# A new order of work, and one scaling moved to ScalarE, in a two-part image block on one NeuronCore

## The chip, the cores and the metric

One core of a Trainium2 chip runs the whole program. The metric is the device time of one execution in microseconds (us), lower is better.

## The reference

The input `x` holds 8 images of 256 channels by 32 x 32 pixels, in fp32. Each image goes through two parts, and images don't depend on one another.

```
conv part:   n   = (x - mean over channels) / sqrt(var + 1e-6)
             qkv = W_qkv n                                  (768 rows)
             agg = pointwise(depthwise 5x5(qkv))            (768 rows)
             per head of 8 rows, raw qkv and agg alike:
               q, k = relu(...);  kv = k^T [v, 1];  out = (q kv) / (q k^T 1)
             y   = x + batchnorm(W_proj out)
token part:  t   = layernorm of y over channels, per pixel
             w   = expert weights of the image: mean over pixels -> router -> softmax -> top 2
             out = y + sum_e w_e (gelu(t W1_e + b1_e) W2_e + b2_e)   (6 experts of width 341)
```

So the expert weights `w` of an image need its whole conv part, its second norm and a small router, and no second product of the token part can be made without them.

## The kernel before

Channels lie on the 128 partitions, an image is two tiles of 1024 pixels. The 768 rows of qkv are six tiles: 0 and 1 are q, 2 and 3 are k, 4 and 5 are v.

**Engines.** TensorE (PE) does every product. fp32 precision in the large products comes from splitting both sides into an fp16 high part and an fp16 low part: three fp16 products in place of one. ScalarE (ACT) empties every PSUM bank of the products, one by one. VectorE (DVE) does the depthwise 5x5 convolution as "taps", one SCALAR_TENSOR_TENSOR for each of most taps and each tile, in the tile order (2, 3), (4, 5), (0, 1): 132 operations for the first image, 138 for each other one. The remaining ("base") taps of a tile are scaled by ACT and added by GpSimd (POOL, L875 and L881). POOL also does the norms' sums, reciprocal roots and products, the scaling of the attention output, the low parts, and additions into the output. SyncE (SP) loads and stores.

**Order.** `schedule()` writes one list of items, `ORDER`, and PE, ACT, POOL and SP each walk it from front to back and do their part of each item, with semaphores between them. So an item that waits on one engine holds back everything behind it on that engine. Two PSUM banks take turns: a product may fill a bank only when ACT has emptied the product two places before. The items of one image are:

- `squares`, `sums`, `stats`, `rnorm`, `rbc`, `apply`, `high`, `low`: a norm (number 0 of the input, 1 of the token part), with two tiles or two halves each. `stats` are 32 PE products of one column, `rbc` spreads the result to all partitions, `apply` multiplies on POOL, `high` and `low` split the result.
- `qkv`: tile and pixel half. `base`: a base tap. `agg`: the pointwise product after the taps.
- `tok` (transposes of raw k and v), `kv`, `mask`, `att`, `scale`, `back`: the attention, half 0 from raw qkv, half 1 from the aggregated tiles. `proj`: the projection with the addition to `x`.
- `logits`, `exp`: the router. `ffn`: the first product of one of 32 feed-forward blocks (2 pixel halves by 16 groups of 128 hidden rows), with gelu. `gsplit`: the hidden rows times their expert weight, split into high and low. `second`: the second product of a block, `LAG` = 3 blocks behind its `ffn`. `final`: what a pixel half gives to the output.

DVE doesn't walk the list. It runs the taps of all images, and between taps with certain numbers it does small tasks: the reciprocals of the attention's denominators (`rden`), and the router's maximum (`max`) and expert weights (`route`). Each waits for other engines, and the taps behind it wait too:

```
OF_LAST = {14: ("rden", 1, 0), 20: ("rden", 1, 1), 74: ("max",), 84: ("route",)}
OF_THIS = {94: ("rden", 0, 0), 100: ("rden", 0, 1)}
```

OF_LAST belongs to the image before the one whose taps run, OF_THIS to that image itself. A period here is the time from the `agg` of tiles 0 and 1 of one image to that of the next. In a middle period (image number j), the list before holds, in short: agg of tiles 0, 1; attention half 1; qkv tiles 0, 1 of the next image; proj; tok; second norm; kv and mask; logits; then the input norm of the next image, attention half 0, agg and qkv of tiles 2 to 5 and kv half 1. Of the 32 ffn blocks of each period 15 stand ahead of the logits and 17 behind.

Of the kernel before, what the change touches and what calls it, by code (L numbers as in the profile page):

```python
# [31 lines left out]
P = 128  # L32
B, C, HH, WW = 8, 256, 32, 32
T = HH * WW
CT = C // P
# [44 lines left out]
def schedule():  # L80

    o = []
    waiting = []
    stream = [(s, f) for s in range(B) for f in range(NCH * FT)]
    todo = list(stream)
    given = set()

    def give(it):
        o.append(it)
        given.add(it)  # L90
# [7 lines left out]
    def fill(k, s):  # L98
        for _ in range(k):
            if not todo or todo[0][0] > s:  # L100
                return
            i = len(stream) - len(todo)
            n = todo.pop(0)
            assert ("low", n[0], 1) in given
            give(("ffn",) + n)
            if i > 0:
                assert ("exp", stream[i - 1][0]) in given
                give(("gsplit",) + stream[i - 1])
            if i >= LAG:
                second(i - LAG)  # L110

    def based(items, n=1):
        for it in items:
            give(it)
            for b in waiting[:n]:
                give(b)
            del waiting[:n]

    def rest():
        for b in waiting:  # L120
            give(b)
        waiting.clear()

    def qkv(s, a, n=1):
        for m in (a, a + 1):
            based([("qkv", s, m, c) for c in range(NCH)], n)
            waiting.extend(("base", s, m, i) for i in range(base_taps(s, m)))

    def agg(s, a, n=1):
        based([("agg", s, m, c) for m in (a, a + 1) for c in range(NCH)], n)  # L130

    for j in range(-1, B + 2):
        d, c, a = 0 <= j < B, 1 <= j <= B, 0 <= j + 1 < B
        old, new = j - 2, j - 1
        n = 3 if j == 0 else 1
        if c:
            agg(new, 0)
            fill(1, old)
            for t in range(TT):
                based([("att", new, 1, t)])  # L140
                if t % 2:
                    fill(1, old)
            give(("scale", new, 1))
        if d:
            qkv(j, 0, n)
        if c:
            fill(1, old)
            based([("back", new, 1, ch, g) for ch in range(NCH) for g in range(2)])
            fill(1, old)
            based([("proj", new, ch, m) for ch in range(NCH) for m in range(CT)])  # L150
            give(("squares", new, 1))
            give(("sums", new, 1))
        if d:
            give(("relu_q", j))
            for t in range(TT):
                based([("tok", j, t)], n)
                if t % 2:
                    fill(1, old)
        if c:
            based([("stats", new, 1, 0)])  # L160
            give(("rnorm", new, 1))
            fill(2, old)
            based([("rbc", new, 1, ch) for ch in range(NCH)])
            give(("apply", new, 1))
            fill(2, old)
            give(("high", new, 1))
            give(("low", new, 1))
        if d:
            based([("kv", j, 0, g) for g in range(2)], n)
            give(("mask", j, 0))  # L170
        if c:
            based([("logits", new)])
        fill(NCH * FT, old)
        if a:
            give(("squares", j + 1, 0))
            give(("sums", j + 1, 0))
        if j == -1:
            give(("weights", 0))
        if c:
            give(("exp", new))  # L180
        fill(2, new)
        if a:
            based([("stats", j + 1, 0, i) for i in range(2)])
            give(("rnorm", j + 1, 0))
            fill(2, new)
            based([("rbc", j + 1, 0, ch) for ch in range(NCH)])
            give(("apply", j + 1, 0))
        if j == -1:
            give(("weights", 1))
        if d:  # L190
            for t in range(TT):
                based([("att", j, 0, t)], n)
                if t % 2:
                    fill(1, new)
            give(("scale", j, 0))
        if a:
            give(("high", j + 1, 0))
            give(("low", j + 1, 0))
        fill(2, new)
        if d:  # L200
            based([("back", j, 0, ch, g) for ch in range(NCH) for g in range(2)], n)
            rest()
            agg(j, 2)
            fill(1, new)
        if a:
            qkv(j + 1, 2)
            fill(1, new)
        if d:
            agg(j, 4)
            fill(1, new)  # L210
        if a:
            qkv(j + 1, 4)
            fill(1, new)
        if d:
            based([("kv", j, 1, g) for g in range(2)])
            give(("mask", j, 1))
        rest()
    k = len(stream)
    assert not todo
# [5 lines left out]

ORDER = schedule()
# [16 lines left out]
def norm_before():  # L243

    runs = [(it[1], it[2]) for it in ORDER if it[0] == "squares"]
    return dict(zip(runs[1:], runs))
# [22 lines left out]
def build(nc, x, w_qkv, w_dw, w_pw, w_proj, bn, bn_rows, w_router, w1, b1, w2, b2, parts, out):  # L269
    with ExitStack() as ctx:  # L270
# [134 lines left out]
        def drained(it):  # L405

            return FILL[it] + 1
# [723 lines left out]
```

## Time and profile before

| | |
|---|---|
| median of 3 runs | 1727.04 us (1724.31 to 1729.64) |
| the profiled execution | 1725.51 us, of which 1723.6 us span |
| instructions | 18116 |
| busy, PE | 1403.7 us (81%) |
| busy, DVE | 1303.4 us (76%) |
| busy, POOL | 1187.4 us (69%) |
| busy, ACT | 915.0 us (53%) |
| mean granted TensorE clock | 0.90 of full speed |
| load of one image, issue to landing | 5.0 us (median) |

The span runs from the first to the last instruction. A busy time is the time in which the engine had at least one instruction running. The granted clock has two levels, full (2.4 GHz) and half (1.2 GHz), and a stretch shows their mean. L487 and L500 are the lines of the split products (`ffn` and `qkv`; `second`), L534 and L539 those of `agg`, L1067 that of the taps.

### The profile page before, as it was taken

How to read it: one execution, taken by the hardware profiler on the slowest of the kernel's cores; microseconds unless marked ns; L12 is line 12 of the kernel's file. 1: busy time of each engine (PE TensorE's matmuls, PEld its weight loads, DVE VectorE, ACT ScalarE, POOL GpSimd, SP SyncE). 2: the span in 40 equal slices, each digit the busy share in tenths (PEclk: the TensorE clock that was granted, in tenths of full speed). 3: DMA queues.
4: the chain of work that ended last, by engine and by line, in shares of the span. 5: the costliest groups of instructions: out<-in, count | busy, mean ns of one | idle time of the engine just before them, and what ended most of it. 6: DMA issues, size and time to landing. Idle time of an engine off the chain costs nothing.

```text
span 1723.6 us, 18116 instructions
## 1 busy us (share of the span) xinstructions
PE 1403.7 (81%) x6652; PEld 771.5 (45%) x6652; DVE 1303.4 (76%) x1305; ACT 915.0 (53%) x1606; POOL 1187.4 (69%) x1017
## 2 busy tenths in 40 slices
PE   4344865988889878988889878988889879768998
PEld 2133534544545435544545435544445435534443
DVE  4999999889589895889589895889589895920000
ACT  3452642565557644665557645565557645433554
POOL 3673554877697758876697758876697757535776
PEclk7666986999999989999999989999999989988999
DMA  5100000000010000100010000100010000100000
GB/s 173 74 0 25 1 0 0 25 1 13 1 62 1 13 1 0 62 1 13 1 60 3 13 1 1 61 1 13 1 37 1 13 0 1 37 0 13 1 13 25
DMA packets 14247, 32.70 MB, mean 19 GB/s; under 512 B 2384, under 2 KB 5328, under 8 KB 13904
## 3 DMA queue, kind: packets, MB, share of 16 engines
q1 hardware_dynamic: 14160, 31.56, 5.2%
q8 instruction: 52, 0.85, 0.2%
q14 instruction: 35, 0.29, 0.1%
HBM read 23.17 MB, written 8.39 MB: 18 GB/s over the span
## 4 chain that ended last, share of the span: by engine, by line
PE 44%; DVE 23%; POOL 16%; ACT 10%; issue 6%; DMA 1%; POOLq 0%; SPq 0%; DVEq 0%
DVE dacc L1067 19%; PE wbk L487 16%; PE acc L500 12%; PE wbk L580 6%; POOL dwo L881 4%; POOL gl L915 3%; POOL hb L912 3%; ACT tapb L655 2%; POOL yr L905 2%; PE wbk L589 2%; PE wbk L534 2%; POOL nrm L838 1%; PE wbk L539 1%; PE wbk L554 1%; PE wbk L566 1%
## 5 line engine op out<-in xcount | busy, mean ns | idle before, releaser
L1067 DVE SCALAR_TENSOR_TENSOR dacc<-qkvs,dww,dacc 128x930 f32<-128x930 f32 (+4 forms) x954 | 1052.3, 1185 | 0.0
L912 POOL TENSOR_SCALAR hb<-hb,ewg 128x512 f32<-128x512 f32 x256 | 189.8, 742 | 252.2 <-ACT gh L677 252.1
L915 POOL TENSOR_TENSOR gl<-hb,gh 128x512 f16<-128x512 f32 x256 | 306.3, 1196 | 21.4
L770 ACT ACTIVATE hb<-wbk,b1s 128x512 f32<-128x512 f32 x256 | 175.4, 686 | 244.4 <-PE wbk L487 243.8
L881 POOL TENSOR_TENSOR dwo<-dwo,tapb 128x992 f32<-128x992 f32 (+1 forms) x104 | 237.4, 2283 | 46.7 <-ACT tapb L655 39.5
L487 PE MATMUL wbk<-th,w1h 128*128 128x512 f16 x512 | 163.8, 403 | 69.7 <-ACT vt L743 36.7
L500 PE MATMUL acc<-gh,w2h 128*128 128x512 f16 x512 | 200.6, 392 | 19.4 <-POOL gl L915 19.3
L677 ACT ACTIVATE gh<-hb,ewg 128x512 f16<-128x512 f32 x256 | 182.3, 712 | 40.7 <-DVE ewg L1020 40.7
L500 PE MATMUL acc<-gl,w2h 128*128 128x512 f16 x512 | 200.0, 391 | 0.0
L500 PE MATMUL acc<-gh,w2l 128*128 128x512 f16 x512 | 199.8, 390 | 0.0
L487 PE MATMUL wbk<-tl,w1h 128*128 128x512 f16 x512 | 162.3, 400 | 0.0
L487 PE MATMUL wbk<-th,w1l 128*128 128x512 f16 x512 | 160.7, 397 | 0.0
L655 ACT ACTIVATE tapb<-qkvs,dww 128x1024 f32<-128x1024 f32 x104 | 118.0, 1144 | 72.8 <-POOL dwo L881 66.6
L977 DVE MAX8 mx<-lg 128x8 f32<-128x16 f32 x8 | 1.4, 176 | 168.2 <-ACT lg L767 168.2
L971 DVE RECIPROCAL den<-den 128x128 f32<-128x128 f32 x32 | 30.4, 951 | 98.0 <-ACT den L750 97.6
L487 PEld LDWEIGHTS wbk<-th,w1h 128*128 128x128 f16 x512 | 42.6, 102 | 133.6 <-ACT vt L743 42.3
L500 PEld LDWEIGHTS acc<-gh,w2h 128*128 128x128 f16 x512 | 51.4, 100 | 91.0 <-POOL gl L915 29.3
L487 PE MATMUL wbk<-xh,wqh 128*128 128x512 f16 x192 | 59.0, 390 | 40.7 <-ACT qkvs L727 20.9
L534 PE MATMUL wbk<-dwo,pw 128*128 128x512 f32 x64 | 44.4, 836 | 53.5 <-ACT qr L734 32.4
L727 ACT ACTIVATE qkvs<-wbk 128x512 f32<-128x512 f32 x96 | 56.9, 593 | 53.0 <-PE wbk L487 52.8
L861 POOL TENSOR_TENSOR kt<-kt,den 128x1024 f32<-128x1024 f32 x32 | 62.5, 1971 | 32.3 <-DVE den L971 32.3
L487 PEld LDWEIGHTS wbk<-tl,w1h 128*128 128x128 f16 x512 | 52.5, 102 | 67.9 <-issue 13.2
(147 smaller groups left out, 2388.7 us busy)
## 6 DMA issues: line engine op xcount, KB each, us to landing
xa<-x SPq DMA_DIRECT2D x8, 1024.0 KB, 5.0
yr<-x SPq DMA_DIRECT2D x8, 1024.0 KB, 5.0
out<-yr SPq DMA_DIRECT2D x16, 512.0 KB, 2.8
dwo<-w SPq DMA_DIRECT2D x1, 2048.0 KB, 10.9
yr<-w SPq DMA_DIRECT2D x2, 1024.0 KB, 16.0
dwo<-w_qkv SPq DMA_DIRECT2D x1, 768.0 KB, 4.7
wp<-w_proj SPq DMA_DIRECT2D x1, 512.0 KB, 12.1
pw<-w_pw SPq DMA_DIRECT2D x16, 24.0 KB
```

What stands on the lines that cost most here:

```text
L487: last = nc.tensor.matmul(dst, w[:, k, m * P:(m + 1) * P], d[:, k, c * CH:(c + 1) * CH], start=(i == 0), stop=(i == len(parts) - 1))
L500: last = nc.tensor.matmul(acc[:, m, :], w[:, t, m * P:(m + 1) * P], d[:, f % GB, :], start=(t == 0 and i == 0), stop=(t == FT - 1 and i == 2),
L534: last = nc.tensor.matmul(b[:], pw[:, m, :], dwo[:, m, c * CH:(c + 1) * CH], start=True, stop=True)
L580: last = nc.tensor.matmul(b[:], wp[:, k, m * P:(m + 1) * P], (ac, qr)[k // CT][:, k % CT, c * CH:(c + 1) * CH], start=(k == 0), stop=(k == ...
L655: ins = nc.scalar.activation(tapb[:, i % 2, :], qkvs[:, m, :], ACT.Copy, scale=w)
L677: nc.scalar.activation(gh[:, f % GB, :], hb[:, f % GB, :], ACT.Copy, scale=w).then_inc(g_high, 1)
L770: last = nc.scalar.activation(hb[:, f % GB, :], b[:], ACT.Gelu, bias=b1s[:, f % FT:f % FT + 1], scale=1.0 / (X_SCALE * W_SCALE))
L861: nc.gpsimd.tensor_tensor(v, v, r, ALU.mult).then_inc(att_scaled[h], 1)
L881: ins = nc.gpsimd.tensor_tensor(d3[:, oy, ox], d3[:, oy, ox], t3[:, iy, ix], ALU.add)
L912: nc.gpsimd.tensor_scalar(hb[:, f % GB, :], hb[:, f % GB, :], ewg[s % 2][:, f % FT:f % FT + 1], 0.0, ALU.mult, ALU.add).then_inc(g_scaled, 1)
L915: nc.gpsimd.tensor_tensor(gl[:, f % GB, :], hb[:, f % GB, :], gh[:, f % GB, :], ALU.subtract).then_inc(g_low, 1)
L1067: ins = nc.vector.scalar_tensor_tensor(out=dst[:, oy, ox], in0=i3[:, jy, jx], scalar=dww[:, m, tap:tap + 1], in1=a3[:, oy, ox], op0=ALU.mu ...
```

## The change

The list is written anew. DVE's tasks move to other tap numbers, `high`, `low`, `squares`, `relu_q`, `apply` and `scale` become items of one tile or half, and one operation changes its engine.

1. The tapped image's way to its routing goes ahead. Of the 32 blocks of a period 9 stand ahead of the logits (5 of them between `agg` and `proj`, where 7 stood) and 23 behind. The loop keeps `KEEP` = 9 blocks of an image for the next period.
2. Attention half 0 of the image whose taps run, up to its `att`, `scale` and the items beside them, and `qkv` tile 2 of the next image move ahead of the logits. `back` of half 0 stands right behind them.
3. The input norm is begun two images ahead of the tapped one, where it was one ahead: `squares` to `apply` stand between the first blocks after `exp`, each group with one block, and `high` and `low` wait until the next period, beside `proj` and `tok`. In the first image the norm of image 1 stands among the base taps, ahead of attention half 0.
4. After the logits two blocks stand ahead of `exp`, then `agg` of tiles 2, 3. One block stands between single `agg`, `qkv`, `kv` and base items.
5. `gsplit`: POOL's multiplication of `hb` by the expert weight (L912) goes to ACT, behind the one that makes `gh`. POOL keeps the subtraction (L915).
6. DVE's tasks: `rden` of half 1 at taps 10 and 14, `rden` of half 0 at 58 and 64, `max` at 72, `route` at 80.

```diff
+    def give(*items, n=1):
+        for it in items:
+            o.append(it)
+            given.add(it)
+            if it[0] in BANKED and n > 1:
+                base(n)
+    def base(n):
+        o.extend(waiting[:n])
+        del waiting[:n]
+    def rest():
+        base(len(waiting))
+    def add_base(s, a):
+        waiting.extend(("base", s, m, i) for m in (a, a + 1) for i in range(base_taps(s, m)))
...
+    def fill(k):
         for _ in range(k):
...
+            if todo and ("low", todo[0][0], 1, CT - 1) in given and (("exp", todo[0][0]) in given or todo[0][1] < 2):
+                i = len(stream) - len(todo)
+                give(("ffn",) + todo.pop(0))
+                while unsplit and ("exp", unsplit[0][0]) in given:
+                    give(("gsplit",) + unsplit.pop(0))
+                unsplit.append(stream[i])
+                if i >= LAG:
+                    second(i - LAG)
+            base(1)
...
+    def norm_in(s):
+        return [[("squares", s, 0, 0)], [("squares", s, 0, 1), ("sums", s, 0)],
+                [("stats", s, 0, 0)], [("stats", s, 0, 1), ("rnorm", s, 0)],
+                [("rbc", s, 0, 0), ("rbc", s, 0, 1)], [("apply", s, 0, 0)], [("apply", s, 0, 1)]]
+    def norm_out(s):
+        return [[("high", s, 0, 0)], [("low", s, 0, 0), ("high", s, 0, 1)], [("low", s, 0, 1)]]
...
+    for j in range(B + 1):
+        d, c, a, f = j < B, j >= 1, j + 1 < B, j + 2 < B
+        new, nxt = j - 1, j + 1
         n = 3 if j == 0 else 1
         if c:
...
+            give(*agg(new, 0), *agg(new, 1))
+            fill(1)
             for t in range(TT):
...
+                give(("att", new, 1, t))
+                if t == 3:
+                    fill(1)
+                    give(("scale", new, 1, 0))
+            give(("scale", new, 1, 1))
+        if j == 0:
+            for group in norm_in(1)[:2]:
+                give(*group)
         if d:
...
+            give(*qkv(j, 0), *qkv(j, 1), n=n)
+            add_base(j, 0)
+            if j == 0:
+                for group in norm_in(1)[2:]:
+                    give(*group, n=n)
+        out = norm_out(nxt) if a else [[], [], []]
         if c:
...
+            fill(2)
+            give(*[("back", new, 1, ch, g) for ch in range(NCH) for g in range(2)])
+            fill(1)
+            give(("proj", new, 0, 0), *out[0])
+            give(("proj", new, 0, 1))
+            give(("proj", new, 1, 0), *out[1])
+            give(("proj", new, 1, 1))
+        else:
+            give(*out[0], *out[1])
+        toks = [("tok", j, t) for t in range(TT)] if d else []
+        give(*toks[:2], n=n)
+        if c:
+            if not d:
+                fill(2)
+            give(*out[2], ("squares", new, 1, 0))
+            give(*toks[2:4])
+            give(("squares", new, 1, 1), ("sums", new, 1))
+            give(*toks[4:])
+        else:
+            give(*out[2], *toks[2:], n=n)
         if d:
...
+            give(("relu_q", j, 0))
+            give(("kv", j, 0, 0), ("kv", j, 0, 1), n=n)
+            give(("mask", j, 0), ("relu_q", j, 1))
         if c:
...
+            fill(1)
+            give(("stats", new, 1, 0), ("rnorm", new, 1))
+            fill(1)
         if d:
...
+            give(*[("att", j, 0, t) for t in range(4)], n=n)
         if c:
...
+            fill(1 if d else 2)
+            give(("rbc", new, 1, 0), ("rbc", new, 1, 1), ("apply", new, 1, 0), ("apply", new, 1, 1))
+        if d:
+            give(("scale", j, 0, 0))
+            give(*[("att", j, 0, t) for t in range(4, TT)], n=n)
         if c:
+            give(("high", new, 1, 0))
+            fill(1 if d else 2)
+            give(("high", new, 1, 1))
+        if d:
+            give(("scale", j, 0, 1))
+        if c:
+            give(("low", new, 1, 0), ("low", new, 1, 1))
+            if a:
+                give(*qkv(nxt, 2))
+            give(("logits", new))
+        if d:
+            give(*[("back", j, 0, ch, g) for ch in range(NCH) for g in range(2)], n=n)
+        if c:
+            if a:
+                give(*qkv(nxt, 3))
+            else:
+                fill(1)
+            fill(left(new - 1) + 2)
             give(("exp", new))
...
+        rest() if j == 0 else None
         if d:
...
+            give(*agg(j, 2), *agg(j, 3))
+            if a and c:
+                add_base(nxt, 2)
+        if j == 0:
+            give(*qkv(1, 2), *qkv(1, 3))
+            add_base(1, 2)
         if d:
...
+            for group in norm_in(j + 2) if f else [[]] * 4:
+                give(*group)
+                fill(1)
+            fill(1)
+            give(*agg(j, 4))
+            fill(1)
+            give(*agg(j, 5))
+            fill(1)
+            if a:
+                for m in (4, 5):
+                    for it in qkv(nxt, m):
+                        give(it)
+                        fill(1)
+                add_base(nxt, 4)
+            else:
+                fill(4)
+            give(("kv", j, 1, 0))
+            fill(2)
+            give(("kv", j, 1, 1))
+            fill(1)
             give(("mask", j, 1))
...
+            while left(new) > KEEP and new >= 0:
+                fill(1)
...
+KEEP = 9
...
                     nc.scalar.activation(gh[:, f % GB, :], hb[:, f % GB, :], ACT.Copy, scale=w).then_inc(g_high, 1)
+                    nc.scalar.activation(hb[:, f % GB, :], hb[:, f % GB, :], ACT.Copy, scale=w).then_inc(g_scaled, 1)
...
-                    pool.wait_ge(g_high, no)
-                    pool.sem_inc(pool_gate, 1)
-                    nc.gpsimd.tensor_scalar(hb[:, f % GB, :], hb[:, f % GB, :], ewg[s % 2][:, f % FT:f % FT + 1],
-                                            0.0, ALU.mult, ALU.add).then_inc(g_scaled, 1)
                     pool.wait_ge(g_scaled, no)
...
-            OF_LAST = {14: ("rden", 1, 0), 20: ("rden", 1, 1), 74: ("max",), 84: ("route",)}
-            OF_THIS = {94: ("rden", 0, 0), 100: ("rden", 0, 1)}
+            OF_LAST = {10: ("rden", 1, 0), 14: ("rden", 1, 1), 72: ("max",), 80: ("route",)}
+            OF_THIS = {58: ("rden", 0, 0), 64: ("rden", 0, 1)}
```

## Rows read from the trace of the kernel before

**Rows 1.** The page's part 4, the chain of work that ended last, by engine.
```profile
PE 44%; DVE 23%; POOL 16%; ACT 10%; issue 6%; DMA 1%; POOLq 0%; SPq 0%; DVEq 0%
```

**Rows 2.** Windows: us, then busy us of each engine (instructions), PEclk, DMA share, GB/s.
```profile
754.60:949.10 194.50, 171.08 (x831) 93.34 (x830) 161.97 (x162) 111.67 (x199) 145.80 (x125) 0.94 0.05 17
...
1338.20:1519.30 181.10, 141.41 (x699) 78.98 (x697) 155.83 (x160) 88.28 (x167) 110.98 (x102) 0.91 0.04 12
...
1519.30:1723.60 204.30, 184.62 (x794) 87.47 (x794) 5.52 (x21) 95.50 (x160) 137.59 (x135) 0.94 0.03 11
```

**Rows 3.** Timeline of PE: start, us, line, operation, [idle before <-releaser].
```profile
202.06 1.96 PE L534 MATMUL wbk<-dwo,pw 128*128 128x512 f32 x4 [2.19 <-DVE dwo L1053]
...
366.23 1.88 PE L534 MATMUL wbk<-dwo,pw 128*128 128x512 f32 x4
...
754.58 1.88 PE L534 MATMUL wbk<-dwo,pw 128*128 128x512 f32 x4
...
761.57 3.78 PE L534 MATMUL wbk<-dwo,pw 128*128 128x512 f32 x4 [5.11 <-ACT qr L734]
...
859.66 0.51 PE L599 MATMUL wbk<-rws,us 128*128 128x11 f32 x4
...
1519.26 6.51 PE L534 MATMUL wbk<-dwo,pw 128*128 128x512 f32 x8 [18.93 <-DVE dwo L1053]
```

**Rows 4.** Timeline of DVE in the period from 754.6 us.
```profile
775.14 6.70 DVE L1067 SCALAR_TENSOR_TENSOR dacc<-qkvs,dww,dacc 128x961 f32<-128x961 f32 x6
...
813.00 28.78 DVE L1067 SCALAR_TENSOR_TENSOR dacc<-qkvs,dww,dacc 128x900 f32<-128x900 f32 x26
...
860.53 0.18 DVE L977 MAX8 mx<-lg 128x8 f32<-128x16 f32 x1 [18.75 <-ACT lg L767]
...
861.07 11.10 DVE L1067 SCALAR_TENSOR_TENSOR dacc<-qkvs,dww,dacc 128x961 f32<-128x961 f32 x10
...
880.47 4.40 DVE L1067 SCALAR_TENSOR_TENSOR dacc<-qkvs,dww,dacc 128x930 f32<-128x930 f32 x4
```

**Rows 5.** Groups of one period: xcount | busy, mean ns | idle before.
```profile
L677 ACT ACTIVATE gh<-hb,ewg 128x512 f16<-128x512 f32 x32 | 22.8, 713 | 5.4 <-DVE ewg L1020 5.4
...
L912 POOL TENSOR_SCALAR hb<-hb,ewg 128x512 f32<-128x512 f32 x32 | 24.1, 752 | 27.9 <-ACT gh L677 27.9
...
L915 POOL TENSOR_TENSOR gl<-hb,gh 128x512 f16<-128x512 f32 x32 | 38.7, 1210 | 2.7
...
L881 POOL TENSOR_TENSOR dwo<-dwo,tapb 128x992 f32<-128x992 f32 x12 | 27.5, 2295 | 5.6 <-ACT tapb L655 5.0
...
L566 PE MATMUL wbk<-kvm,qr 128*128 128x144 f32 x64 | 9.5, 289 | 0.1
...
L554 PE MATMUL wbk<-vt,kt 128*128 128x129 f32 x64 | 7.5, 275 | 0.0
...
L547 PE MATMUL wbk<-ident,qkvs 128*128 128x128 f32 x32 | 4.5, 277 | 0.3 <-ACT sum_b L756 0.3
```

**Rows 6.** The chain of the same period in order of time: start, us.
```profile
823.39 2.74 PE wbk L487 x6
...
831.40 1.29 PE acc L500 x6
...
840.61 3.46 PE wbk L589 x32
...
884.37 1.65 POOL sv L826
```

**Rows 7.** Timelines of DVE and POOL in the first two images.
```profile
118.25 37.34 DVE L1067 SCALAR_TENSOR_TENSOR dacc<-qkvs,dww,dacc 128x900 f32<-128x900 f32 x34
...
124.51 0.45 POOL L851 TENSOR_TENSOR kvm<-kvr,blk 128x128 f32<-128x128 f32 x1 [7.27 <-ACT kvr L745]
...
285.69 11.09 DVE L1067 SCALAR_TENSOR_TENSOR dacc<-qkvs,dww,dacc 128x961 f32<-128x961 f32 x10
...
300.00 4.40 DVE L1067 SCALAR_TENSOR_TENSOR dacc<-qkvs,dww,dacc 128x930 f32<-128x930 f32 x4
```

More of the change, by code:

```diff
@@ L96, in second @@
             give(("final", s, n // FT))
-    def fill(k, s):
+    def fill(k):
         for _ in range(k):
[L100 to L130, printed above, removed]
@@ new lines, in norm_out @@
+    def norm_out(s):
+        return [[("high", s, 0, 0)], [("low", s, 0, 0), ("high", s, 0, 1)], [("low", s, 0, 1)]]
+    give(("squares", 0, 0, 0), ("squares", 0, 0, 1), ("sums", 0, 0), ("weights", 0), ("stats", 0, 0, 0),
+         ("stats", 0, 0, 1), ("rnorm", 0, 0), ("rbc", 0, 0, 0), ("rbc", 0, 0, 1), ("apply", 0, 0, 0),
+         ("apply", 0, 0, 1), ("weights", 1), ("high", 0, 0, 0), ("low", 0, 0, 0), ("high", 0, 0, 1), ("low", 0, 0, 1))
+    give(*[it for m in range(2, QT) for it in qkv(0, m)])
@@ L135, in schedule @@
+    add_base(0, 2)
+    add_base(0, 4)
+    for j in range(B + 1):
+        d, c, a, f = j < B, j >= 1, j + 1 < B, j + 2 < B
+        new, nxt = j - 1, j + 1
         n = 3 if j == 0 else 1
         if c:
-            agg(new, 0)
-            fill(1, old)
+            give(*agg(new, 0), *agg(new, 1))
+            fill(1)
             for t in range(TT):
[L140 to L143, printed above, removed]
@@ L144, in schedule @@
-        if d:
-            qkv(j, 0, n)
-        if c:
[L147 to L152, printed above, removed]
-        if d:
[L154 to L158, printed above, removed]
@@ L159, in schedule @@
-        if c:
[L160 to L167, printed above, removed]
+                give(("att", new, 1, t))
[3 more added lines that the diff above has]
+            give(("scale", new, 1, 1))
@@ L179, in schedule @@
-        if c:
-            give(("exp", new))
[L181 to L189, printed above, removed]
-        if d:
[L191 to L199, printed above, removed]
-        if d:
[L201 to L215, printed above, removed]
+            fill(1 if d else 2)
@@ L223, in schedule @@
     return o
+KEEP = 9
+BANKED = ("qkv", "agg", "kv", "stats", "rbc", "att", "back", "proj", "tok", "logits", "ffn")
 ORDER = schedule()
-BANKED = ("qkv", "agg", "kv", "stats", "rbc", "att", "back", "proj", "tok", "logits", "ffn")
 FILL = {it: n for n, it in enumerate([it for it in ORDER if it[0] in BANKED])}
@@ L243, in norm_before @@
 def norm_before():
-    runs = [(it[1], it[2]) for it in ORDER if it[0] == "squares"]
+    runs = [(it[1], it[2]) for it in ORDER if it[0] == "squares" and it[3] == 0]
     return dict(zip(runs[1:], runs))
@@ L441, in _ @@
             for it in ORDER:
[L442 removed]
+                if it[0] == "apply" and it[2:] == (0, CT - 1) and it[1] + 1 < B:
                     s = it[1]
```

107 lines of the change are left out of this document (48 added, 59 removed).

## The prediction

> **What bounds the kernel now.** I read the chain first, then windows of one period each, then the timelines. The chain [rows 1] changes hands: PE holds 44% of it, DVE 23%, POOL 16%, ACT 10%. No engine is the bound by itself, and a period is a loop of waits. The windows say the same [rows 2]: in a middle period of 194.5 us PE is busy 171.1 us, DVE 162.0, POOL 145.8, ACT 111.7, at a mean granted clock of 0.94. The starts of the agg of tiles 0 and 1 [rows 3] give the frame: image 0 at 202.1, image 1 at 366.2, then steps of 194.5 (949.1 in rows 2), then 181.1 for the last to 1519.3, and 204.3 to the end.
>
> Where the loop is closed shows in DVE's timeline [rows 4]. MAX8 at 860.5 waited 18.8 us for the logits, which PE made at 859.7, 105 us after its agg at 754.6 [rows 3]. Ten taps follow (11.1 us), and the route block lasts until 880.5, 8.3 us. ACT's gsplit waits for it (5.4 us in the row of L677 [rows 5]), and with it the second products. From there to the next agg it is 68.6 us. So 105 + 21 + 69 us is the period: whoever shortens the way from agg to logits gains until another wait ends last.
>
> **Prices.** Six matmuls of 512 columns take 1.29 us at the full clock, so a block (ffn and second) takes PE 2.58 us, and a qkv chunk 1.29 [rows 6]. At the half level, after PE stood idle, the same six take 2.74 with their end [rows 6]. An fp32 pass of four instructions takes 1.88 us with its end, some 1.72 without [rows 3]: agg of tiles 0 and 1 is 3.8 us, proj eight such, 13.8. A norm's stats take 3.5 us [rows 6]; the attention's products 9.5 us for 16 att, 7.5 for both kv, 4.5 for 8 tok, so 2.3 for four back [rows 5].
>
> **The scaling on ACT.** It isn't in the trace. The nearest row is the gh operation on the same tile, 0.71 us [rows 5]; its bounds are 0.6 (overlap with its neighbours) and 0.75 (what POOL took). It adds 32 x 0.65 = 21 us to ACT's 112 in a period, and takes 24 from POOL's 146. ACT at 133 us of some 187 is not the bound. What it buys lies elsewhere: a block's way from gelu to gl is as long as before (0.71 + 1.16 in place of 0.75 + 1.21), but POOL gets free in a crowded stretch.
>
> **From agg to DVE's task at tap 58.** Ahead of the first four att of half 0 PE has, in the new list: agg 3.8, 7 blocks 18.1, 12 att 7.1, 4 qkv chunks 5.2, back 2.3, proj 13.8, tok 4.5, kv 3.7 (one half), stats 3.5. Sum 62.0. Waits: two PSUM banks and ACT's queue ahead of back (gelu, gh, the new scaling, a base tap) 2; ahead of tok's third the squares, which now wait for low of the next image: proj's last drain and addition, then a low on POOL like an add of L881 (2.3 us [rows 5]), then two squares between the tok drains: 6, and 1 for the clock; 1 for the last drain. So these att are drained 72 us after the agg. DVE is there earlier: it waits at tap 10 for the attention half 1 until 9.6, and then has 4 taps, two reciprocals and 44 taps, which is tap 58 at 64 (taps 14 to 74 take 66.6 in rows 4, from 775.1 to 841.8). It waits 8 us.
>
> **From tap 58 to the weights.** 1.0 (reciprocal) + 6.7 (6 taps) + 1.0 + 8.9 (8 taps) puts the maximum at 89.6 us; the logits are ready by my count at 86 (two more blocks, norm product, high, two qkv chunks), so their 18.8 us of waiting are gone. Then 0.5 + 8.9 (8 taps) + the route block. It took 8.3 us in rows 4 and 3.3 us in image 0 (296.8 to 300.0 [rows 7]), where POOL had no work in it; in the middle periods POOL was in the norm's sums. In the new list those stand behind gsplit, which needs the weights, so POOL is idle there: I take 3.4, with 8.3 as the other end. Weights at 102.4 us, against 126 before. *The port.* The Trainium skill (SBUF — State Buffer, Who interferes with whom) says that VectorE's tensor_scalar in its two-port mode, or an operation with two SBUF inputs, and a GpSimd operation that reads SBUF shut each other out for a whole instruction. By it the block would be 3.3 us with POOL idle and about 8.3 with POOL in long operations; the two blocks of this trace agree.
>
> **From the weights to the next agg.** Before PE's first second product with them come gh, hb and gl: 2.7 us. Then 39 half blocks 50.3, stats 3.5, rbc (one pass) 1.7, agg of tiles 4 and 5 taken as that of 0 and 1, 3.8, 4 qkv chunks 5.2, kv 3.7: 68.2. POOL has two gl (2.4), two output additions of half a tile (about half of an L881 add each, 2.5) and the norm's sums (two of that size, 4.7 [rows 5]) ahead of stats: they end 8.8 us after the weights, where PE is at 4.0: 4.8 of waiting. Then POOL has a gl and a base add (2.3) with each block, 3.5 us against PE's 2.6, and rnorm (1.65 for the power [rows 6], a product of full size and three small steps, 4.6): rbc waits some 4. These two gaps put the clock down: 2 + 2.6. Sum 2.7 + 68.2 + 4.8 + 4 + 4.6 = 84.3. The period is 102.4 + 84.3 = 186.7; bounds 178 (POOL's two waits hidden) and 195 (route block 8.3, and 3 us more for handovers).
>
> **The ends.** *Image 0:* DVE was busy through it. Its attention half 0 was done long ahead of tap 94; now tap 58, at about 122.7 [rows 7], needs it. The mask came at 124.5, after 7.3 us of waiting for kv [rows 7], so POOL was done with the base adds at 117.2. It now has the next image's norm among and behind them: sums 4.7, rnorm 4.6, apply (two products like an add of L881) 4.7, which makes 131.2, then high 1. Only then come tok and kv, with nothing else for PE and so at the half clock, 7 and 6.5: I get the mask at 147 and the att at 151, so DVE waits 28 us: agg at 230, not 202 (bounds 0 and 35). *Period 1* holds 23 blocks behind its weights instead of 14. DVE has no wait ahead of them: 84 + 0.5 + 8.9 + 3.4 = 97, + 84.3 = 181: 411. *Periods 2 to 5:* 4 x 186.7 = 747: 1158. *Period 6* has no input norm: 5.2 of PE's work, its two waits and their clock go, 102.4 + 2.7 + 63 + 1 = 169: 1327. *Period 7* has no qkv either (5.2) and no low ahead of tok (6): 96 + 2.7 + 58 = 157, which is also DVE's own work (162 less the 5 of the route block); with handovers 160: 1487, against 1519. *The end:* 204.3 us with 54 blocks to finish; now 41. 13 x 2.58 = 33.5 less, but the last image's chain has 9 blocks of cover for 22, and the weights come when no block is left: + 7 there (route after exp, 5 us, and the clock 2). 178: 1665.
>
> Span 1665, and 1.9 between span and time as in the profiled execution, whose 1725.5 is 1.5 under the median of the runs: **1667 us**, 3.5% faster.
>
> **DMAs.** Each input load is issued behind the last apply of its image and waited for a whole period later; the output stores and loads stand at their old places by the final items. They cost nothing while a load (5.0 us to landing in the table ahead) has more than 100 us of cover.
>
> **The rivals.** *A, the covers work:* sums, rnorm and apply on POOL end in time, and PE doesn't wait there. For it speaks that POOL loses 24 us a period, against it the count above. 178 in 4 periods and 173 in the first: 1667 - 35 - 8 = 1624. *B, only the ends gain:* the route block stays at 8.3 and each handover of two banks costs 0.2 more: period 195, + 33 + 8: 1708. *C, slower:* the attention of the tapped image is late for tap 58. Each us that it is later than my 72 is a us of all of periods 1 to 5, since nothing else of the loop is slack there but PE, which waits too. The 60 us of gain are used up by 12 us a period: att drained at 84 decides. Fifteen us late would give 1742. For it: the chain ACT to POOL to ACT at tok is new, and PE at half the clock would make 62 us of work longer quickly; against it: before, the logits, which lie behind more work, took 105. *D, nothing changes* (within 0.3%, which is about what a measurement of this kernel can tell from no change): gains and the new waits of image 0 and period 1 (+28, +17) cancel.
>
> *The clock.* Before, PE's row at 823.4 shows half-level durations behind an idle stretch [rows 6], and the period's mean is 0.94; I expect 0.93 to 0.96. The Trainium skill (TensorE: Matmul & The Clock Gate, HAM oscillation) warns that idle gaps which recur with each tile cost the slow start each time; it would speak for C, and the rows price a start at 2 to 3 us.
>
> **How the numbers follow.** Forecast (1635 to 1690) 0.55, A 0.15, B 0.18, C 0.09, D 0.03. The range holds forecast, A and B with their bounds: 1612 to 1715. Faster 0.88, same 0.03, slower 0.09.
>
> **What would show it.** Right: MAX8 waits under 2 us and the rden at tap 58 about 8; the route block 3.4 us; PE waits for POOL at stats and rbc in the middle of a period; DVE waits some 28 us at tap 58 of image 0; 41 blocks behind the last agg. Wrong: a rden wait over 20 us in each period (C), no POOL waits of PE (A), or the route block at 8 us (B). What would most easily make the number wrong is the handovers between ACT and PE, of which I count only the large ones.

## The result, and the profile after

The changed kernel takes 1746.78 us (median of 4 runs, 1745.71 to 1749.76) against 1727.11 for the kernel before in the same comparison: 1.0117 times as long, with a 95% interval of 1.0097 to 1.0137. I had forecast 1667. The profiled execution has a span of 1745.5 us, 21.9 more than before, and a mean granted clock of 0.894.

The page's part 4, and three groups of its part 5:

```profile
PE 43%; POOL 26%; ACT 11%; DVE 11%; issue 8%; DMA 1%; POOLq 0%; SPq 0%; ACTq 0%; DVEq 0%
...
L956 POOL TENSOR_TENSOR gl<-hb,gh 128x512 f16<-128x512 f32 x256 | 302.3, 1183 | 493.2 <-ACT hb L725 492.5
...
L1012 DVE RECIPROCAL den<-den 128x128 f32<-128x128 f32 x32 | 30.5, 952 | 269.6 <-ACT den L798 269.3
...
L725 ACT ACTIVATE hb<-hb,ewg 128x512 f32<-128x512 f32 x256 | 182.0, 711 | 0.0
```

Beside [rows 1] the chain has lost half of DVE (23% to 11%) and has gained as much of POOL (16% to 26%), although POOL does less work in all than before (1005.5 us busy for 1187.4). The group of L1012 shows that DVE now waits 270 us in the run for the attention, where it waited 98 before.

Windows of the changed kernel: a middle period, its parts up to the weights and behind them, and the last three periods (the columns are those of [rows 2]):

```profile
816.70:1018.10 201.40, 175.42 (x829) 98.21 (x828) 158.95 (x161) 130.98 (x232) 123.76 (x93) 0.92 0.05 16
816.70:923.30 106.60, 96.65 (x458) 57.46 (x457) 84.39 (x93) 66.77 (x136) 60.95 (x43) 0.92 0.00 1
923.30:1018.10 94.80, 78.77 (x373) 40.75 (x372) 74.56 (x69) 64.21 (x97) 62.81 (x50) 0.93 0.09 34
...
1219.50:1404.20 184.70, 165.31 (x794) 91.61 (x793) 159.85 (x161) 126.91 (x226) 113.39 (x84) 0.94 0.03 12
1404.20:1572.10 167.90, 153.14 (x745) 86.12 (x744) 146.02 (x151) 109.27 (x204) 84.48 (x69) 0.94 0.04 13
1572.10:1745.50 173.40, 150.79 (x639) 71.80 (x638) 5.42 (x21) 103.25 (x176) 83.47 (x66) 0.93 0.03 9
```

The middle period is 201.4 us, not the 186.7 of the forecast, and not the 194.5 of before [rows 2]. PE does the same products in it, but is busy 4.3 us longer and idle 2.6 us longer (26.0 for 23.4). The extra busy time is matmuls at the half clock: the mean granted clock of the period fell from 0.94 to 0.92, which is some 4 us of 200 (an estimate from these two figures).

By periods, from one agg of tiles 0 and 1 to the next:

| stretch | before | forecast | measured |
|---|---|---|---|
| to the agg of image 0 | 202.1 | 230 | 230.8 |
| to that of image 1 | 164.1 | 181 | 183.1 |
| four middle periods, each | 194.5 | 186.7 | 201.4 |
| the next | 194.5 | 169 | 184.7 |
| the last | 181.1 | 160 | 167.9 |
| the end | 204.3 | 178 | 173.4 |

Against before the first two cost 48 us and the middle 28, and the last three give back 54. Against the forecast nearly everything is in the middle: 59 of the 80 us, and 16 and 8 in the two periods behind it, which are built alike.

PE in the changed kernel, at its starts of agg (230.80, 413.89, 816.71) and at its larger waits of the middle period (the bracket is the idle time before the row and what ended it):

```profile
230.80 4.39 PE L582 MATMUL wbk<-dwo,pw 128*128 128x512 f32 x5 [23.10 <-DVE dwo L1094]
...
413.89 2.40 PE L582 MATMUL wbk<-dwo,pw 128*128 128x512 f32 x5
...
816.71 3.69 PE L582 MATMUL wbk<-dwo,pw 128*128 128x512 f32 x8
...
867.27 4.01 PE L595 MATMUL wbk<-ident,qkvs 128*128 128x128 f32 x16 [3.08 <-ACT vt L791]
872.12 5.93 PE L602 MATMUL wbk<-vt,kt 128*128 128x129 f32 x32 [0.84 <-ACT vt L791]
...
929.28 0.38 PE L548 MATMUL acc<-gh,w2h 128*128 128x512 f16 x1 [2.86 <-ACT sum_b L758]
...
934.80 3.55 PE L637 MATMUL wbk<-mean_w,rb 128*128 128x1 f32 x16 [4.07 <-POOL rb L858]
...
942.35 1.84 PE L637 MATMUL wbk<-mean_w,nrm 128*128 128x1 f32 x16
...
951.09 3.22 PE L643 MATMUL wbk<-rb,spread 128*128 128x512 f32 x4 [4.28 <-POOL rb L876]
...
1012.53 0.39 PE L548 MATMUL acc<-gh,w2h 128*128 128x512 f16 x1 [2.43 <-POOL gl L956]
```

The price of a wait shows twice: the bracket is the wait itself, and the row shows what follows it at the half clock. Stats take 3.55 us at 934.8 for the 1.84 of the second sixteen at 942.4, rbc 3.22 for 1.88, kv 5.93 for 3.7.

DVE in the changed kernel:

```profile
149.64 0.95 DVE L1012 RECIPROCAL den<-den 128x128 f32<-128x128 f32 x1 [29.85 <-ACT den L798]
...
825.85 0.95 DVE L1012 RECIPROCAL den<-den 128x128 f32<-128x128 f32 x1 [29.39 <-ACT den L798]
...
892.90 0.95 DVE L1012 RECIPROCAL den<-den 128x128 f32<-128x128 f32 x1 [12.12 <-ACT den L798]
...
910.19 0.17 DVE L1018 MAX8 mx<-lg 128x8 f32<-128x16 f32 x1
...
919.98 0.16 DVE L1027 RECIPROCAL rt<-rt 128x1 f32<-128x1 f32 x1 [0.36 <-ACT rt L751]
...
923.31 8.84 DVE L1108 SCALAR_TENSOR_TENSOR dacc<-qkvs,dww,dacc 128x930 f32<-128x930 f32 x8
...
934.62 5.53 DVE L1100 SCALAR_TENSOR_TENSOR dacc<-qkvs,dww,dwo 128x1024 f32<-128x1024 f32 x2
...
986.62 2.49 DVE L1100 SCALAR_TENSOR_TENSOR dacc<-qkvs,dww,dwo 128x1024 f32<-128x1024 f32 x2
```

The 18.8 us at MAX8 [rows 4] are gone and the route block is 3.3 us (919.98 to 923.31), so the weights come 106.6 us after the agg, where it was 126. But at 825.85 DVE has a wait of 29.4 us for half 1 that was 5.7 before: it has run ahead and waits one agg later. That is the first sign that its wait isn't what closes the loop.

### The profile page after: what moved, and what is told of

Read it like the earlier page. It is cut to its first block, busy times and chain, and to the rows that moved or that the text cites. A ratio compares the mean times of both kernels' runs of the same rounds, so it can differ in the third digit from the quotient of the medians.

```text
span 1745.5 us, 17861 instructions
## 1 busy us (share of the span) xinstructions
PE 1427.3 (82%) x6652; PEld 797.3 (46%) x6652; DVE 1285.1 (74%) x1305; ACT 1070.7 (61%) x1863; POOL 1005.5 (58%) x761
## 4 chain that ended last, share of the span: by engine, by line
PE 43%; POOL 26%; ACT 11%; DVE 11%; issue 8%; DMA 1%; POOLq 0%; SPq 0%; ACTq 0%; DVEq 0%
PE wbk L535 16%; PE acc L548 10%; DVE dacc L1108 8%; POOL dwo L926 8%; POOL gl L956 5%; PE wbk L628 5%; PE wbk L602 4%; POOL nrm L885 3%; PE wbk L637 2%; ACT hb L725 2%; ACT gh L724 2%; ACT hb L818 1%; PE wbk L587 1%; PE wbk L582 1%; POOL kt L906 1%
## 5 line engine op out<-in xcount | busy, mean ns | idle before, releaser
L956 POOL TENSOR_TENSOR gl<-hb,gh 128x512 f16<-128x512 f32 x256 | 302.3, 1183 | 493.2 <-ACT hb L725 492.5
L818 ACT ACTIVATE hb<-wbk,b1s 128x512 f32<-128x512 f32 x256 | 175.4, 685 | 184.3 <-PE wbk L535 183.8
L926 POOL TENSOR_TENSOR dwo<-dwo,tapb 128x992 f32<-128x992 f32 (+1 forms) x104 | 241.7, 2324 | 15.1 <-ACT tapb L703 12.1
L1012 DVE RECIPROCAL den<-den 128x128 f32<-128x128 f32 x32 | 30.5, 952 | 269.6 <-ACT den L798 269.3
L725 ACT ACTIVATE hb<-hb,ewg 128x512 f32<-128x512 f32 x256 | 182.0, 711 | 0.0
L643 PE MATMUL wbk<-rb,spread 128*128 128x512 f32 x64 | 44.0, 825 | 57.6 <-POOL rb L876 57.6
L1100 DVE SCALAR_TENSOR_TENSOR dacc<-qkvs,dww,dwo 128x1024 f32<-128x1024 f32 x46 | 90.3, 2006 | 0.0
L614 PE MATMUL wbk<-kvm,qr 128*128 128x144 f32 x512 | 80.4, 301 | 9.1 <-ACT rb L813 3.2
L595 PE MATMUL wbk<-ident,qkvs 128*128 128x128 f32 x256 | 49.8, 348 | 42.3 <-ACT vt L791 37.3
## 6 DMA issues: line engine op xcount, KB each, us to landing
wp<-w_proj SPq DMA_DIRECT2D x1, 512.0 KB, 12.1
```

The source lines that it names most:

```text
L614: last = nc.tensor.matmul(b[:, g * RD:(g + 1) * RD], qr[:, g, t * P:(t + 1) * P], kvm[:, g, :], start=True, stop=True)
L725: nc.scalar.activation(hb[:, f % GB, :], hb[:, f % GB, :], ACT.Copy, scale=w).then_inc(g_scaled, 1)
L818: last = nc.scalar.activation(hb[:, f % GB, :], b[:], ACT.Gelu, bias=b1s[:, f % FT:f % FT + 1], scale=1.0 / (X_SCALE * W_SCALE))
L926: ins = nc.gpsimd.tensor_tensor(d3[:, oy, ox], d3[:, oy, ox], t3[:, iy, ix], ALU.add)
L956: nc.gpsimd.tensor_tensor(gl[:, f % GB, :], hb[:, f % GB, :], gh[:, f % GB, :], ALU.subtract).then_inc(g_low, 1)
L1100: ins = nc.vector.scalar_tensor_tensor(out=dacc[:, m % 2, :], in0=qkvs[:, m, :], scalar=w, in1=dwo[:, m, :], op0=ALU.mult, op1=ALU.add)
```

## Experiments

**Theory 1:** PE's own list closes the period. Its length is PE's work, plus each wait in the list, plus the half-clock stretch behind each wait; DVE and the weights have slack. **Theory 2** (rival C of the prediction): the late attention half 0 holds DVE at tap 58, and DVE's wait holds the agg.

**1. Later DVE tasks.** The changed kernel with later tap numbers:

```diff
-OF_LAST = {..., 72: ("max",), 80: ("route",)}
-OF_THIS = {58: ("rden", 0, 0), 64: ("rden", 0, 1)}
+OF_LAST = {..., 76: ("max",), 84: ("route",)}
+OF_THIS = {66: ("rden", 0, 0), 72: ("rden", 0, 1)}
```

> Only DVE's task numbers move: rden of half 0 from taps 58 and 64 to 66 and 72, max from 72 to 76, route from 80 to 84. DVE's wait for the attention (12.1 us in each middle period of the changed kernel) shrinks to about 3 us. Theory 1 (what sets the time of the weights is exp on ACT, which stands behind two blocks and ends at 919.9 us when DVE's tap 80 is at 919.6; DVE's wait costs nothing by itself): weights at the same time after the agg (106.6 us), whole time the same within 0.3%, 1742 to 1752. Theory 2 (rival C of the prediction taken by itself: each us of waiting at tap 58 is a us of the period): 9 us less in five periods, 1702 or less.

Measured: 1751.68 us, 1.0143 times the time before (1.0111 to 1.0175). The same three waits of DVE in this kernel:

```profile
828.45 0.95 DVE L1012 RECIPROCAL den<-den 128x128 f32<-128x128 f32 x1 [37.81 <-ACT den L798]
...
895.02 0.95 DVE L1012 RECIPROCAL den<-den 128x128 f32<-128x128 f32 x1 [2.76 <-ACT den L798]
...
909.30 0.18 DVE L1018 MAX8 mx<-lg 128x8 f32<-128x16 f32 x1 [1.27 <-ACT lg L815]
```

The wait of 12.1 us fell to 2.8 and the one at half 1 grew from 29.4 to 37.8. The period did not shrink (202.5), and the time stayed in theory 1's range. Theory 2 falls.

**2. Weights earlier as well.** The same, with the router's exp ahead of its two blocks:

```diff
-            fill(left(new - 1) + 2)
-            give(("exp", new))
+            fill(left(new - 1))
+            give(("exp", new))
+            fill(2)
```

> The late tap numbers, and exp ahead of the two blocks that stand between logits and exp. Theory 1 (exp behind blocks on ACT is late): the weights come 5 to 6 us earlier after the agg, near 101 us. If PE's way behind the weights starts with them, each of five periods gains 5 us: 1720. If POOL's sums of the next norm bound that way and can't start earlier, the gain stays under 2 us a period: 1737 or more. Theory 2 (DVE's wait at tap 58): no more than with the late tap numbers alone, 1702.

Measured: 1748.40 us, 1.0137 (1.0111 to 1.0164). The weights came at 103.5 us, 3 earlier than in the changed kernel and not the 5 to 6 forecast; the stretch behind them, which now has the two blocks in it, grew from 94.7 to 97.9, and the period stayed at 201.4. So the weights don't close the loop either: only the division of PE's list by them has moved.

**3 and 4. The two halves of the change.** Number 3 is the changed kernel with the scaling on POOL again. Number 4 is the kernel before with the scaling on ACT and nothing else:

```diff
                     nc.scalar.activation(gh[...], hb[...], ACT.Copy, scale=w).then_inc(g_high, 1)
+                    nc.scalar.activation(hb[...], hb[...], ACT.Copy, scale=w).then_inc(g_scaled, 1)
...
-                    pool.wait_ge(g_high, no)
-                    pool.sem_inc(pool_gate, 1)
-                    nc.gpsimd.tensor_scalar(hb[...], hb[...], ewg[...], 0.0, ALU.mult, ALU.add).then_inc(g_scaled, 1)
```

> The scaling of hb goes back from ACT to POOL, everything else as changed. Theory 1 (behind the weights POOL is the bound with gl, sums, base adds and rnorm): POOL has 0.7 us more per block in that stretch, 6 blocks up to rbc, 4 to 8 us a period more, 1770 to 1790. Theory 3 (the loss comes from ACT, which carries 21 us more in a period and empties banks later): the kernel gets faster than 1747, at least down to the time before, 1727.

> The kernel before with the scaling of hb on ACT alone. Theory 1: POOL's queue ahead of the agg and behind it (base adds behind gsplit) gets shorter, ACT is at 133 of 194 us: faster by 1 to 4 us a period, 1700 to 1720. Theory 3 (ACT's queue is what hurts): slower than 1727, by up to 20 us.

| median us | scaling on POOL | scaling on ACT |
|---|---|---|
| order before | 1725.17 | 1689.77 |
| new order | 1771.10 | 1746.78 |

**Theory 3**, in the expectations, was that ACT's longer queue is what hurts. Both runs speak against it: ACT without the scaling made the new order slower, in the range of theory 1, and ACT with it made the old order faster, by more than the 7 to 27 us that theory 1 had for it. Their ratios to the kernel before are 1.0263 (1.0236 to 1.029) for number 3 and 0.9797 (0.9772 to 0.9823) for number 4. The scaling gives 35 us in the order before and 24 in the new one; the order by itself costs 46 with the scaling on POOL and 57 with it on ACT (1746.78 is from another comparison, whose kernel before took 1727.11). Two rows of number 4, a window of one period and DVE's wait in it:

```profile
931.40:1119.20 187.80, 170.22 (x831) 94.12 (x830) 159.44 (x162) 129.27 (x231) 123.91 (x93) 0.95 0.05 17
```

```profile
1034.17 0.18 DVE L974 MAX8 mx<-lg 128x8 f32<-128x16 f32 x1 [18.05 <-ACT lg L768]
```

The period fell by 6.7 us while MAX8's wait stayed at 18. Its PE waits fell: above 0.3 us each they sum to 16.6 us where before they summed to 21.5 and in the changed kernel to 24.4. Those for gl (3.1 us before) are gone, and those at ACT's drains are some 2.6 us shorter.

**5. Sums early.** In the changed kernel the input norm's squares and sums go right behind exp, ahead of the drains of agg 2, 3 and of the two gsplits (and are taken out of their old place):

```diff
             give(("exp", new))
+            if d and f:
+                for group in norm_in(j + 2)[:2]:
+                    give(*group)
```

> The squares and sums of the norm two images ahead stand right behind exp, ahead of agg of tiles 2 and 3, where POOL waits 9.5 us for the weights; before they stood behind the first gsplit. Theory 1 (PE's wait of 4.1 us for the sums and of 4.3 us for rnorm behind the weights lengthen the period): both shrink, 4 to 6 us in each of periods 2 to 5 and some in period 1: 1720 to 1731. Rival (POOL is the bound later anyway, or the sums take the port while DVE works on the weights, which come up to 3 us later): gain under 1 us a period, 1742 or more.

Measured: 1733.07 us, 1.0038 (1.0024 to 1.0052), 13.7 less than the changed kernel, period 197.9. That is 3.5 us a period, between the ranges of the two. The wait at stats is gone, but POOL's next link is late instead, as PE's row shows (4.28 us before):

```profile
942.70 3.75 PE L646 MATMUL wbk<-rb,spread 128*128 128x512 f32 x4 [6.74 <-POOL rb L879]
```

**6. The norm spread.** As number 5, and each later link of the chain gets more cover: stats and rnorm behind the first block, rbc two blocks later, each apply with a block of its own.

```diff
-            for group in norm_in(j + 2) ...:
-                give(*group)
-                fill(1)
+                fill(1)
+                give(*norm_in(j + 2)[2], *norm_in(j + 2)[3])
+                fill(2)
+                for group in norm_in(j + 2)[4:]:
+                    give(*group)
+                    fill(1)
+                fill(1)
```

> The changed kernel with the input norm spread otherwise, in periods 2 to 5: squares and sums right behind exp, stats and rnorm behind the first block, rbc two blocks later, then apply with a block each. The number of blocks ahead of and behind the logits stays. Theory 1 (the changed kernel loses behind the weights, since each step of the norm has one block of 2.6 us as cover and POOL needs 5 to 8 us for it): PE's two waits of 4.1 and 4.3 us and the half clock behind them go, 8 to 12 us a period in four or five periods: period 190 to 193, 1700 to 1712. Rival (POOL's total work in that stretch is what counts, wherever the steps stand): the waits come back at the second products, period 197 or more, 1730 or more.

Measured: 1697.64 us, 0.9837 (0.9818 to 0.9855). A window of one period, and PE at the places of the former waits (stats, rbc):

```profile
788.00:979.20 191.20, 170.99 (x829) 94.51 (x829) 162.41 (x161) 130.25 (x232) 124.73 (x93) 0.95 0.05 17
```

```profile
902.47 1.03 PE L547 MATMUL wbk<-th,w1h 128*128 128x512 f16 x2 [1.30 <-ACT st L820]
...
911.57 0.60 PE L547 MATMUL wbk<-th,w1h 128*128 128x512 f16 x2 [0.70 <-ACT rb L825]
```

The period is 10.2 us shorter, with PE idle 20.2 us in place of 26.0 and busy 4.4 less. The same work is done by the same engines; only places in the list moved. This is most of what the new order had lost in a middle period: 13.6 against number 4. The period is in theory 1's range and the time 2 us below it, though a part of the rival is there too: PE's waits for gl at the second products grew from 4.8 to 6.3 us.

**7. Image 0's tasks at their old taps.**

```diff
+ of_this = OF_THIS if s > 0 else {94: ("rden", 0, 0), 100: ("rden", 0, 1)}
```

> For the first image alone the reciprocals of attention half 0 go back to taps 94 and 100. Theory (DVE's wait of 29.9 us at tap 58 of the first image is lost for the whole run, since its taps are the path until the first agg): agg at 201 to 204 us, and 25 to 29 us less in all: 1720. Rival (the first blocks' period then waits for something else of the image, POOL's queue with scale ahead of the base adds): half of it or less, 1733 or more.

Measured: 1737.32 us, 1.006 (1.0043 to 1.0077). The agg of image 0 starts at 214.8, 16 us earlier, not 28, and of the 16 only 9.5 are left in the whole time, since period 1 takes 188.5 us for 183.1. DVE isn't what holds this agg any more: it ended the taps of image 0 at 198.7. PE comes to it late by its own list, in which the chain of the norm of image 2 stands ahead of it with no block as cover (in the changed kernel these waits lay ahead of the 23.1 us for DVE and cost nothing), and its second half then waits for ACT:

```profile
185.57 3.54 PE L637 MATMUL wbk<-mean_w,rb 128*128 128x1 f32 x16 [5.32 <-POOL rb L858]
...
197.55 3.38 PE L643 MATMUL wbk<-rb,spread 128*128 128x512 f32 x4 [5.03 <-POOL rb L876]
...
223.48 3.78 PE L582 MATMUL wbk<-dwo,pw 128*128 128x512 f32 x4 [6.58 <-ACT qr L782]
```

So with DVE's wait gone the first stretch is set as the middle periods are, by the waits in PE's list. The rival of the expectation had the size right; it named POOL's queue behind scale, and PE waits for POOL's norm.

**8. Numbers 6 and 7 together**, and the base taps of tile 4 listed two blocks earlier:

```diff
+ waiting.extend(("base", nxt, m, i) for i in range(base_taps(nxt, m)))   # behind each qkv(nxt, m), m = 4, 5
- add_base(nxt, 4)
```

> As the spread norm, and the base taps of tile 4 begin two blocks earlier, and the first image's reciprocals at taps 94 and 100. Theory 1: the wait of 2.4 us and the half clock at the end of each period go too (4 us in six periods) and 10 us at the start: 1665 to 1690, which would be about the time of the old order with the scaling on ACT (1690). Rival: the base adds then collide with apply and final on POOL, no more than the 10 us of the start on top of the spread norm.

Measured: 1676.84 us, 0.9714 (0.9695 to 0.9732). The middle period is 191.2, as in number 6, so the earlier base taps moved nothing there; the last two periods before the end are 4.0 and 3.0 us shorter than in number 6 (180.0 for 184.0, 164.9 for 167.9), where theory 1 had 4 in each of six. The agg of image 0 is at 217.6, 14 us earlier. This is the changed order at its best, and with the same scaling it is 13 us faster than the order before (number 4, 1689.77): its middle periods are still some 3 us longer each and its first two 26 us together, but its last three stretches are 50 us shorter. What the new order gains at the end is real.

**9. The order before, with number 4's scaling and the wait at tok covered.** The second norm's squares and sums, and relu_q, go behind the first tok items:

```diff
-            give(("squares", new, 1))
-            give(("sums", new, 1))
         if d:
-            give(("relu_q", j))
             for t in range(TT):
                 based([("tok", j, t)], n)
                 if t % 2:
                     fill(1, old)
+                if t == 1 and c:
+                    give(("squares", new, 1))
+                    give(("sums", new, 1))
+            give(("relu_q", j))
```

> The kernel before with the scaling on ACT, and squares and sums of the second norm behind the first two tok and a block instead of ahead of them, relu of q behind all tok. PE's wait of 5.2 us at the first block between tok (ACT busy with two squares and two relu ahead of the tok drains) and 2.6 us of half clock behind it are to go. If PE's waits add up to the period one by one: 5 to 8 us less in six periods, 1645 to 1660. Rival (stats then waits for the sums, since they are made later): the wait moves there, 1680 or more.

Measured: 1658.76 us, 0.9615 (0.9597 to 0.9634), faster than both kernels. A period's window, the wait of PE at tok (5.16 us in number 4), and DVE's at MAX8:

```profile
912.00:1093.00 181.00, 167.00 (x831) 93.83 (x830) 159.35 (x162) 129.14 (x231) 123.79 (x93) 0.96 0.05 18
```

```profile
977.36 0.60 PE L491 MATMUL wbk<-th,w1h 128*128 128x512 f16 x2 [2.27 <-ACT vt L748]
```

```profile
1008.09 0.18 DVE L978 MAX8 mx<-lg 128x8 f32<-128x16 f32 x1 [11.77 <-ACT lg L772]
```

One period of each kernel, side by side (idle is the window less PE's busy time):

| kernel | period | PE busy | PE idle | DVE's wait at max |
|---|---|---|---|---|
| before | 194.5 | 171.1 | 23.4 | 18.8 |
| changed | 201.4 | 175.4 | 26.0 | 0 |
| 3, scaling on POOL | 204.9 | 175.7 | 29.2 | 0 |
| 5, sums early | 197.9 | 172.6 | 25.3 | 0 |
| 6, norm spread | 191.2 | 171.0 | 20.2 | 0 |
| 4, before and scaling | 187.8 | 170.2 | 17.6 | 18.1 |
| 9, that and tok | 181.0 | 167.0 | 14.0 | 11.8 |

From the changed kernel to number 9 the idle time falls by 12.0 us and the busy time by 8.4, for the same products: over this distance a us less of waiting came with 0.7 us less of busy time, nearly all of it half clock (the granted clock went from 0.92 to 0.96). It is no fixed price: from before to number 4 the idle time fell by 5.8 and the busy time by only 0.9, from the changed kernel to number 5 by 0.7 and 2.8. DVE's wait at max doesn't order the table at all. That idle and busy time sum to the period is so by definition; that PE's waits set it is shown by numbers 5, 6 and 9, which moved only places in the list so that named waits of PE went.

## Why the prediction was wrong

**Right.** The wait of image 0 (28 forecast, 29.9 measured) and with it the first agg (230, 230.8); the second agg (411, 413.9); the scaling's 0.71 us row (L725 711 ns), the wait for the logits gone, the route block (3.4, 3.3), the end (178, 173.4). The second agg was luck in part: the weights came 93.4 us after the first agg (324.2), not 97, and the next agg 89.7 behind them, not 84.3. The Trainium skill (SBUF — State Buffer, Who interferes with whom) has VectorE and GpSimd contend for a shared pair of ports, one instruction at a time; the route block of 3.3 us, with no POOL operation in it (POOL has none between 917.9 and 927.4), agrees.

**The failed step is "From the weights to the next agg".** I had 84.3 us and it took 94.7. POOL's two waits were sized well: 4.8 and 4 against 4.07 and 4.28. Missing were three things, which with these 0.45 us less add up to the 10.4 within rounding:

- *The first second product with the weights*, forecast 2.7 us behind them, started at 929.28, 6.0 behind: + 3.3. The accumulator must first be emptied by the last final of the previous image, and that stands in ACT's list behind squares, a table load and both gsplits. ACT's rows in the changed kernel:

```profile
923.07 1.05 ACT L738 ACTIVATE nrm<-xa 128x1024 f32<-128x1024 f32 x1
924.13 1.28 ACT L818 ACT_TABLE_LOAD   x1
...
926.01 0.71 ACT L724 ACTIVATE gh<-hb,ewg 128x512 f16<-128x512 f32 x1
...
928.46 1.25 ACT L758 ACTIVATE sum_b<-acc,ob 128x512 f32<-128x512 f32 x2
```

- *Waits for gl* (1.16, 1.16 and 2.43 us), one behind each apply and one at the period's end, where POOL has base additions, final and mask to do: + 4.75.
- *The clock.* PE was busy 78.8 us. Less 3.1 of work ahead of the first second product and my 68.2 that is 7.5 for the half clock, where I had 4.6: + 2.9. The window's mean clock of 0.93 gives 6.6 of them (an estimate, 0.07 of 94.8).

*From agg to the weights* I was 4.3 us short: the att were drained at 76, not 72, since tok and kv ran at the half clock behind their waits (867.27, 872.12), and so did most of what follows them:

```profile
867.20:892.70 25.50, 24.37 (x122) 18.60 (x123) 13.58 (x11) 14.26 (x33) 14.82 (x15) 0.68 0.00 1
```

At 0.68 this is some 8 us of half clock (an estimate, 0.32 of 25.5), where the forecast of this stretch had 1; its waits were 6.8 us (76.0 less 69.2 busy) and not the 9 besides. So over the whole period the term that I sized worst was the clock: some 8 + 6.6 us, for 1 + 4.6.

**The deeper mistake** is the paragraph on the bound with "So 105 + 21 + 69 us is the period: whoever shortens the way from agg to logits gains until another wait ends last". That chain of waits did exist in the trace, but a wait in it is no proof that it sets the pace. DVE's wait at MAX8 was the slack of an engine with 162 us of work in 194.5; PE walks one list without a choice, and the kernel before had 23.4 us of idle in it. Runs 1 and 2 show that neither DVE's tasks nor the weights' time move the period of the changed kernel, and run 4 that the period of the order before falls with the 18 us still there. (No run moves DVE's tasks alone in the order before; that its wait was slack there rests on runs 4 and 9.) So the 7.8 us that I credited each middle period with weren't to be had by this way, and what the new order did to PE's list there was a loss: a chain that goes ACT, POOL, PE, ACT, POOL, PE with one block of cover (2.6 us of PE) where POOL has 5 to 8 us to do. Its rows on POOL in the changed kernel:

```profile
932.28 2.37 POOL L858 TENSOR_TENSOR rb<-xa 128x1024 f32<-128x1024 f32 x1
934.61 2.35 POOL L860 TENSOR_TENSOR nrm<-nrm 128x1024 f32<-128x1024 f32 x1
936.92 2.14 POOL L956 TENSOR_TENSOR gl<-hb,gh 128x512 f16<-128x512 f32 x1
939.02 3.27 POOL L926 TENSOR_TENSOR dwo<-dwo,tapb 128x992 f32<-128x992 f32 x1
942.95 1.16 POOL L956 TENSOR_TENSOR gl<-hb,gh 128x512 f16<-128x512 f32 x1 [0.67 <-ACT hb L725]
944.07 2.31 POOL L926 TENSOR_TENSOR dwo<-dwo,tapb 128x992 f32<-128x992 f32 x1
...
947.31 1.66 POOL L874 TENSOR_TENSOR sv<-sv,mhalf 128x8 f32<-128x8 f32 x1
949.04 1.90 POOL L876 TENSOR_TENSOR rb<-ident,sv 128x1024 f32<-128x1024 f32 x1
```

**The scaling** got no gain of its own in my sum ("What it buys lies elsewhere"). It is the part that wins: 35 us in the order before. There 5.8 of its 6.7 us a period are shorter waits of PE, for gl and at ACT's drains, and 0.9 is busy time.

**Rival C** forecast the right sign and about the right time (1742), but by a mechanism that run 1 refutes. The attention was 4 us late, not 15. The prediction's last sentence of doubt, that only the large handovers between ACT and PE were counted, was nearer to the truth than any of its rivals: the wait for sum_b and those for gl are such.

**Open.** Number 6 leaves 3.4 us of the period against number 4. The wait for sum_b is gone in it; its largest are four for gl (6.3 us, the longest 2.9) and one of 3.1 at tok, and no run removes them alone. And no run puts the best of both together, number 9's list for the middle periods and the new order's end.

## What to carry to other kernels

When several engines walk one list, add up the idle time of the engine with the most work, wait by wait, with the half-clock stretch behind each; a change is worth what it does to that sum, and the longest wait of another engine may be plain slack. Ask of a wait that is to be removed what the engine would do with the time: if it only waits one step later, there is no gain. A chain of short steps across engines must be given at least as much cover at each link as the slower engine's queue needs there, not one filler block by rule.

## What was unexpected of the hardware

A tap with two inputs in SBUF (L1100; at the other taps the running sum lies in PSUM) and POOL's operations lengthen each other. In DVE's rows above a pair takes 2.49 us at 986.62, where POOL has nothing but for its last 0.2 us, and 5.53 at 934.62; POOL's gl and base addition beside it take 2.14 and 3.27 us for 1.16 and 2.31 alone. In the second norm it is the sums:

```profile
865.48 3.33 POOL L858 TENSOR_TENSOR rb<-yr 128x1024 f32<-128x1024 f32 x1
868.79 3.33 POOL L860 TENSOR_TENSOR nrm<-nrm 128x1024 f32<-128x1024 f32 x1
```

3.33 us each, for 2.37 and 2.35 at 932.28. One tap of the pair by itself shows how:

```profile
934.62 3.43 DVE L1100 SCALAR_TENSOR_TENSOR dacc<-qkvs,dww,dwo 128x1024 f32<-128x1024 f32 x1
```

It starts beside POOL's second sum (934.61, 2.35 us) and ends 1.09 us behind the end of that one, nearly as if its own work had begun only then; POOL's gl, the next, is 0.98 us longer than alone. The Trainium skill (SBUF — State Buffer, Who interferes with whom) says that VectorE with two SBUF inputs contends with a GpSimd operation that reads SBUF, and that the contention is an exclusive lock; the lengths agree. I had applied the rule to the route block alone. Here it puts 1.9 us (0.98 and 0.96) into POOL's queue ahead of the rnorm that PE waits for. That they cost time isn't shown: POOL is idle for 0.67 us right behind them (the row at 942.95), so it had made them up before rnorm.
